# Second-round tiles counted back from the last row, exponentials one beat later, and more identity products in front, in a decoder layer on one Trainium2 core

## The reference

```
x = x + attn(layernorm(x))           # sigmoid q and k, 16 heads of 8, k^T v then q (k^T v); norm, gate, Wo, relu
x = x + xattn(layernorm(x), ctx)     # 16 heads of 64: softmax(q k^T / 8) v, then Wo
x = x + ffn(layernorm(x))            # shared SwiGLU (256 wide) + one of 8 routed SwiGLUs, the one of the largest logit
```

## Time and profile before

| | |
|---|---|
| median of 3 runs | 638.46 us |
| lowest and highest | 635.97 us, 639.41 us |
| the profiled execution | 638.0 us |
| its span, first to last instruction | 636.3 us |
| mean granted TensorE clock | 0.98 |
| PE busy | 584.8 us (92%) |
| ACT busy | 432.4 us (68%) |
| DVE busy | 427.4 us (67%) |
| POOL busy | 311.6 us (49%) |

### The profile page before, as it was taken

How to read it: one execution, slowest core, us unless ns; L and a number is a source line. 1 busy time by engine, 2 the same in 40 slices (tenths; PEclk the granted TensorE clock), 3 DMA queues, 4 the chain that set the end, 5 groups by cost and what they waited for, 6 DMA issues and landing times.

```text
span 636.3 us, 15539 instructions
## 1 busy us (share of the span) xinstructions
PE 584.8 (92%) x5461; PEld 533.8 (84%) x5461; DVE 427.4 (67%) x1183; ACT 432.4 (68%) x1514; POOL 311.6 (49%) x331
## 2 busy tenths in 40 slices
PE   8879999999999999999999999999999997968971
PEld 8767998888889889888988898889899986867971
DVE  4858767776776677676867686768674674865551
ACT  2658778786867686767676877787668766635650
POOL 3544644363446543663366336633752374354543
PEclk9988999999999999999999999999999999999996
DMA  6500000100010001000100000000401112433410
GB/s 156 121 2 13 18 3 1 30 2 2 1 31 18 18 2 31 18 19 1 30 19 18 1 14 18 18 2 1 141 28 38 31 43 68 125 116 105 130 37 8
DMA packets 24956, 23.53 MB, mean 37 GB/s; under 512 B 7007, under 2 KB 22497, under 8 KB 24880
## 3 DMA queue, kind: packets, MB, share of 16 engines
q1 hardware_dynamic: 20368, 14.91, 8.9%
q0 software_dynamic: 2784, 6.32, 2.8%
q10 hardware_dynamic: 1728, 1.32, 0.9%
HBM read 15.03 MB, written 7.95 MB: 36 GB/s over the span
## 4 chain that ended last, share of the span: by engine, by line
PE 59%; ACT 17%; DVE 12%; issue 4%; DMA 2%; POOL 1%; another core or an unknown queue 1%; SPq 1%; ACTq 0%; DVEq 0%; POOLq 0%
PE bank L1314 9%; PE bank L1335 9%; ACT prob L1070 7%; PE bank L1196 7%; PE bank L1324 6%; PE bank L1197 6%; PE bank L1198 6%; PE bank L1346 4%; PE bank L1451 4%; PE bank L1295 2%; PE bank L1203 2%; ACT probT L1076 2%; DVE mneg L842 2%; DMA prob<-in_L_xattn_Wk_dram 2%; ACT L1041 1%
## 5 line engine op out<-in xcount | busy, mean ns | idle before, releaser
L1070 ACT ACTIVATE prob<-bank,mneg 128x128 f32<-128x128 f32 x512 | 182.5, 380 | 92.8 <-DVE mneg L842 92.7
L583 POOL TENSOR_TENSOR prob<-prob,rden 128x512 f32<-128x512 f32 x128 | 130.9, 1043 | 105.9 <-DVE rden L849 105.7
L1070 ACT ACTIVATION_READ_ACCUMULATOR prob<-bank,mneg 128x1 f32 x512 | 111.6, 218 | 0.0
L1076 ACT COPY probT<-bank 128x512 f32<-128x512 f32 x128 | 77.7, 607 | 23.4 <-PE bank L1324 23.0
L842 DVE TENSOR_REDUCE mneg<-bank 128x4 f32<-128x512 f32 x128 | 80.6, 671 | 4.0 <-PE bank L1314 3.1
L1324 PE MATMUL bank<-ident,prob 128*128 128x128 f32 x512 | 79.3, 278 | 3.4 <-POOL prob L583 2.0
L522 POOL TENSOR_TENSOR rstd<-var_eps,neg_half 128x4 f32<-128x4 f32 x24 | 24.7, 1030 | 102.3 <-DVE var_eps L676 102.3
L1324 PEld LDWEIGHTS bank<-ident,prob 128*128 128x128 f32 x512 | 59.7, 143 | 11.4 <-issue 5.5
L1314 PE MATMUL bank<-kT,qT 64*128 64x128 f32 x1024 | 65.8, 278 | 0.3 <-issue 0.3
L859 DVE COPY V<-bank 128x512 f32<-128x512 f32 x62 | 42.7, 689 | 33.2 <-PE bank L1198 31.9
L1314 PEld LDWEIGHTS bank<-kT,qT 64*128 64x128 f32 x1024 | 59.7, 188 | 6.2 <-issue 3.0
(11 more groups left out here) (195 smaller groups left out, 1357.9 us busy)
## 6 DMA issues: line engine op xcount, KB each, us to landing
prob<-routed SPq DMA_DIRECT2D x39, 128.5 KB, 2.1
s_work<-in_x_dram SPq DMA_DIRECT2D x8, 256.0 KB, 3.0
ctx_nat<-in_ctx_dram SPq DMA_DIRECT2D x8, 192.0 KB, 2.5
routed<-blank ACTq DMA_DIRECT2D x8, 128.5 KB
s_work<-in_L_ffn_rt_gate_dram SPq DMA_DIRECT2D x1, 1024.0 KB, 5.5
s_work<-in_L_ffn_rt_up_dram SPq DMA_DIRECT2D x1, 1024.0 KB, 9.5
out_dram<-probT,prob POOLq DMA_INDIRECT x39, 2.6
prob<-in_L_xattn_Wq_dram SPq DMA_DIRECT2D x1, 512.0 KB, 8.4
```

The costliest lines, as they stand in the source:

```text
L583: nc.gpsimd.tensor_tensor(view, view, spread(rden[:, m % 2, c * NC:(c + 1) * NC], 2, S), ALU.mult)\
L1070: last = nc.scalar.activation(prob[:, m % 2, p * S:(p + 1) * S], score_bank[c][:, i * S:(i + 1) * S], ACT.Exp, bias=mneg[:, m % 2, p:p + 1 ...
L1076: nc.scalar.copy(probT[:, m % 2, c * 512:(c + 1) * 512], made(r1, ("T", m, c))[:])\
```

## The change

**Exponentials a beat later.** `exps_of` moves the exponentials of matrix n+1 from beats 0 to 3 of `n` to beats 1 to 3 of `n` and beat 0 of `n+1`; for the last matrix the last two quarters stand in beat 3. ACT's list reads nearly word for word as before, since each beat still has `empty_T` and then four exponentials; what has changed is the quarter that they belong to. DVE takes one quarter's maxima in each beat instead of two in beats 0 and 2, first in beats 1 to 3 and last in beat 0, and its reciprocals go to beat 3 and behind the copies of beat 0. POOL's first two multiplications go from beat 2 to beat 3.

**Second-round tiles.** They are counted back from each region's last row, so that they overlap rows that round 1 has done (written again with equal values) or 128 blank rows in front of the region. The blank rows are written by SP near the front, 9 DMAs where there was 1; the eight of ACT are gone. POOL waits in `write_out(j)` for the write of tile j-4, and at j = 21 for all of round 1.

**ACT in the tiles.** The value that says which expert comes next is read behind the copy, a tile ahead.

**In front**, `stay_awake` gives 9 products instead of 6 in beat 2 of n = -4, and 5 more in beat 3.

```diff
+        def exps_of(n, b):
+            if n + 1 == B - 1 and b == NC - 1:
+                return [(n + 1, NC - 2), (n + 1, NC - 1)]
+            if b > 0:
+                return [(n + 1, b - 1)] * (0 <= n + 1 < B)
+            return [(n, NC - 1)] * (0 <= n < B - 1)
...
# SP
-            sp.dma_start(routed[E * REGION:E * REGION + P, :], blank[:]).then_inc(blank_in, 16)
+            for e in range(E + 1):
+                sp.dma_start(routed[e * REGION:e * REGION + P, :], blank[:]).then_inc(blank_in, 16)
...
             sp.wait_ge(table, TABLE_1)
+            sp.wait_ge(blank_in, 16 * (E + 1))
...
-            sp.wait_ge(blank_in, 16 * (E + 1))
             sp.wait_ge(routed_in[1], 16 * GB * (NG // 2))
...
# POOL
-                    if b == 2 and live(n + 1):
+                    if b == 3 and live(n + 1):
                         norm_probs(n + 1, 0)
                         norm_probs(n + 1, 1)
...
+            def written(j):
+                pool.wait_ge(out_in[j % RING], 16 * (j // RING + 1))
             def write_out(j):
+                if 4 <= j <= ROUND1:
+                    written(j - 4)
+                if j == ROUND1:
+                    for i in range(1, 4):
+                        written(j - 4 + i)
...
# DVE
+                if tiles == ROUND2:
+                    entry(nc.vector.scalar_tensor_tensor(out=first[:, 0:E], in0=ntiles[:], scalar=-float(P),
+                                                         in1=next_row[0:1, :], op0=ALU.mult, op1=ALU.add))
+                    entry(nc.vector.tensor_tensor(stride[:], first[:, 1:], first[:, 0:E], ALU.subtract))
...
-                entry(nc.vector.tensor_tensor(stride[:], first[:, 1:], first[:, 0:E], ALU.subtract))
...
-                    entry(nc.vector.tensor_copy(tail_i[:], next_row[0:1, :]))
...
-                    if b == 0 and live(n):
-                        reciprocal(n, 1)
-                    if (n, b) == (B - 1, 0):
-                        fill_first_table()
-                    if b == 2 and live(n + 1):
+                    if b == 3 and live(n + 1):
                         reciprocal(n + 1, 0)
-                    if b == 2 and live(n + 1):
-                        row_max(n + 1, 2)
-                        row_max(n + 1, 3)
+                    if b > 0 and live(n + 1):
+                        row_max(n + 1, b)
...
+                    if b == 0 and live(n):
+                        reciprocal(n, 1)
+                    if (n, b) == (B - 1, 0):
+                        fill_first_table()
                     if b == 0 and live(n + 1):
                         row_max(n + 1, 0)
-                        row_max(n + 1, 1)
...
# ACT
-            def end_region(e):
-                if e == 0:
-                    act.wait_ge(table, TAILS)
-                tail = act.value_load(tail_i[0:1, e:e + 1], min_val=e * REGION, max_val=e * REGION + TOKENS)
-                act.dma_start(routed[bass.ds(tail, P), :], blank[:]).then_inc(blank_in, 16)
...
-                    if live(n + 1):
-                        exp_chunk(n + 1, b)
+                    for chunk in exps_of(n, b):
+                        exp_chunk(*chunk)
...
+            held = {}
             def copy_weights(j):
                 if j >= 3:
                     act.wait_ge(gu_ready, j - 2)
+                nc.scalar.copy(w4[j % 3], rt_gu[:, bass.ds(held.pop(j) * (2 * I), 2 * I)]).then_inc(w4_in, 1)
+                if j + 1 < TILES:
+                    held[j + 1] = expert_of(j + 1)
...
-                if j in END_STEPS:
-                    end_region(END_STEPS.index(j))
...
# PE
                     if (n, b) == (-4, 2):
-                        stay_awake(6)
+                        stay_awake(9)
+                    if (n, b) == (-4, 3):
+                        stay_awake(5)
```

More of the change, by code:

```diff
@@ L193, in decoder_layer @@
         t_row = sb("t_row", [1, ROUND1])
-        tail_i = sb("tail_i", [1, E], I32)
         row_tab = sb("row_tab", [1, 2, ROUND1], I32)
@@ L353, in decoder_layer @@
         TABLE_STEPS = (7, 8, 10)
-        END_STEPS = range(8, 8 + E)
         S1_BANKS = {"turn x": [(0, "s1_dve")], "project first pair": [(1, "s1_dve"), (2, "s1_dve")],
@@ L428, in decoder_layer @@
         CONSTS = CONSTS_S1 + 14
-        TABLE_1, TAILS, TABLE_2 = 15, 16, 27
+        TABLE_1, TABLE_2 = 14, 27
         gu_bank = score_bank[1:]
@@ L610, in _ @@
             nc.gpsimd.iota(expert_m[:], [[0, GB], [1, E]], base=-E, **ramp).then_inc(consts, 1)
-            nc.gpsimd.iota(next_row[:], [[REGION, E]], base=0, **ramp).then_inc(consts, 1)
+            nc.gpsimd.iota(next_row[:], [[REGION, E]], base=P, **ramp).then_inc(consts, 1)
             nc.gpsimd.memset(blank[:, 0:2 * D], 0.0).then_inc(consts, 1)
@@ L615, in _ @@
             s1(0, "rstd of attention")
-            nc.gpsimd.iota(region[:], [[REGION, E]], base=0, **ramp).then_inc(consts, 1)
+            nc.gpsimd.iota(region[:], [[REGION, E]], base=P, **ramp).then_inc(consts, 1)
             nc.gpsimd.iota(steps[:], [[0, E], [P, TOKENS // P]], base=0, **ramp).then_inc(consts, 1)
@@ L927, in second_table @@
                 if third == 0:
-                    entry(nc.vector.tensor_copy(tail_i[:], next_row[0:1, :]))
-                    assert entries[0] == TAILS
                     entry(nc.vector.tensor_tensor(cnt[:], next_row[0:1, :], first[:, 0:E], ALU.subtract))
@@ L1150, in _, with expert_of @@
                             ffn(g, step)
+            def expert_of(j):
+                if j == ROUND1:
+                    act.wait_ge(table, TABLE_2)
+                half, i = (0, j) if j < ROUND1 else (1, j - ROUND1)
+                return act.value_load(exp_tab[0:1, half, i:i + 1], min_val=0, max_val=E - 1)
+            held = {}
             def copy_weights(j):
@@ L1155, in copy_weights @@
                     act.wait_ge(gu_ready, j - 2)
-                if j == ROUND1:
-                    act.wait_ge(table, TABLE_2)
-                half, i = (0, j) if j < ROUND1 else (1, j - ROUND1)
-                e = act.value_load(exp_tab[0:1, half, i:i + 1], min_val=0, max_val=E - 1)
-                nc.scalar.copy(w4[j % 3], rt_gu[:, bass.ds(e * (2 * I), 2 * I)]).then_inc(w4_in, 1)
+                nc.scalar.copy(w4[j % 3], rt_gu[:, bass.ds(held.pop(j) * (2 * I), 2 * I)]).then_inc(w4_in, 1)
+                if j + 1 < TILES:
+                    held[j + 1] = expert_of(j + 1)
             act.wait_ge(table, TABLE_1)
@@ L1165, in _ @@
             act.wait_ge(wr_in, 16 * 3)
+            held[0] = expert_of(0)
             copy_weights(0)
```

## The result

The changed kernel takes 659.31 us (median; 659.15 to 659.41), the kernel before 638.93 on the same chip (635.97 to 644.00, four runs each). The ratio is 1.032, with an interval of 1.029 to 1.036. The profiled executions have spans of 657.4 and 636.3 us, so 21.1 us are to be found. I look for them with a ruler that costs nothing: the start of T0 (the first turn of a matrix on PE, once in each n), which can be read in both traces, in us.

A forecast was written before the change was run, and what follows sets the result against it. PE was taken to bound the loop, a DMA-ACT-PE chain the tiles, the clock the front. Front -1.4, loop +9.2, tiles -3.6, last steps +0.1 make +4.3 us on 638.0: 642.3, median 642.8; range 631 to 649.

The forecast's parts named there:

- The sign: Whole kernel: the change was forecast to make it slower, by 4.3 us.
- The stall between the halves: Loop, beat 0: PE waits for the fourth quarter's exponentials before the scores' second half; 0.45 to 0.9 us, gross 14.2.
- What vanishes against it: Loop: a later PE finds some present waits over; 5 us taken off, bounds 0 and 9.85.
- rival D: Loop: the copy of V in beat 3 becomes a new wait, some 0.7 us in each of 30 n; 650, chance 0.08.
- The end of the loop: Two quarters of exponentials in beat 3 of n = 30 and the last steps: +0.1 us.
- In front: Ahead of the loop: more identity products raise PE's clock from 0.51 at 34.3 to 37.7 us; -1.4 us, bounds -3 and 0.
- The tiles: Behind the loop: ACT freed of blank DMAs and a table wait; -3.6 us, bounds 0 and -11.
- the first: Tiles: ACT's table wait goes, so PE's step from tile 9 to 10 falls from 3.23 to about 1.5; 1.6 us off.
- the unnamed wait: Tiles: ACT's 4.02 us wait with no releaser named, behind a blank DMA; half of it, 2 us, taken off.
- A: Loop: the stall doesn't bite and the waits vanish; loop -3, the rest -4.9, 630 us, chance 0.14.
- B: Tiles: ACT's unnamed waits, 9.3 us, go with its blank DMAs; tiles -11, 635.4 us, chance 0.12.
- C: Loop nearly neutral: the stall stays but takes up all 9.85 us of idle time; +4, 637.6 us, chance 0.20.

## Why the prediction was right or wrong

The sign was right, the size was not: +4.3 us forecast, about +21 measured, outside the range. Step by step:

**The stall between the halves** was right in place, cause and price. Forecast 0.45, 0 and 0.45 and 0.9 us for the remainders 3, 0, 1 and 2; measured from T0 to T1, +0.53, -0.29, +0.56 and +0.96. The signal that I had guessed at 0.05 us took 0.06. Gross 14.2 us forecast; 16.2 measured, 13.8 from n = 0 to 27 and 2.4 in n = 28 to 30.

**What vanishes against it** was the step that failed. "I take 5" stood for waits that disappear, less nothing for new ones. Measured turn by turn from T0 of n = 0 to T0 of n = 31, 8.5 us vanish and 15.2 us of new waits come, beside the stall: 16.2 + 15.2 - 8.5 is, but for rounding, the 23.0 that the loop lost. (These are sums of the differences between the two kernels over all stretches from one turn to the next: those from T0 to T1 that grew are the stall, the others that grew the new waits.) The step had put 15.2 us at nothing. Where four n lost their 2.28 us, by the starts of the turns:

| stretch | before | after | |
|---|---|---|---|
| T0 to T1, remainders 3, 1, 2 | 18.90 | 20.95 | +2.05, the stall |
| T1 to T2, remainder 2 | 3.28 | 4.31 | +1.03, T2 waits for V |
| T3 to T0, 3 to 0 and 1 to 2 | 6.11 | 6.57 | +0.46, T0 waits for V, for POOL |
| all others | | | -1.26, waits that vanish |

The 8.5 us are more than my 5 and near the upper bound that I had set. Of the 15.2 us, 11.0 lie before n = 28 and 4.2 at the end. I had booked new waits in rival D alone, at 0.08, and there for one copy of V, that of beat 3. The larger wait, at T2, is for the copy of beat 1, where a reduction stands ahead as well, and two blocked instructions of DVE. I had seen that a reciprocal and a reduction stand ahead of V in beat 3, and that POOL's multiplies go a beat later, and costed neither with the slack in hand. That slack could be read for POOL: in remainder 2, before, T0 starts 3.92 us behind POOL's first multiply (325.37 and 329.29). The multiply and the signal need 1.17 of them, which leaves 2.75, and the beat that POOL's multiplies moved by is 3.4 us long there.

**The end of the loop**, from T0 of n = 28 to T0 of n = 31, took 6.6 us. 2.4 of them are the stall, which the 14.2 had in them; the other 4.2, against the +0.1 that I had given, are the waits ahead of the three T0, 3.0 at the last. I had looked at the two quarters in beat 3 and at the scatters' order, not at what stands in POOL's queue ahead of the multiplies when no slack is left: four scatters at 1.27 us each. One edit there gave 2.6 us back, by the profiles.

**In front**: -1.4 forecast. The piece itself gave 1.2, with the clock as foreseen. In the changed kernel it was lost at T0 of n = 0, 0.7 later than before; in the kernel before, by itself, a ratio of 0.998 says that it holds.

**The tiles**: -3.6 forecast, -2.5 on the first chip; on the others, with the old exponentials, the stretch behind T0 of n = 31 went from 92.3 to 91.2 us. Of the two terms, the first was wrong: the step from tile 9 to 10 takes 3.23 us after the change too (579.22 to 582.45), as the product of the shared FFN stands in it (1.95 us, in both kernels). The 2 us for the unnamed wait have no base, since those waits are there without these DMAs on the first chip, and not there with them on another. The real gain was elsewhere, tiles 13 to 18, 9.6 us before and 7.9 with the change, both on chips of the experiments.

**The rivals.** A is refuted: the stall bites, 25 times. B is too. C had the mechanism of the vanishing waits, 8.5 us, and missed the new ones. D had a part of the right cause, too small.

**What stays open**: what the unnamed waits in the tiles of the first chip are; what ACT's delay alone costs with the old order on DVE and POOL; and how much of the wait for V at T2 would stay if only the reduction, or only the blocked instructions, stood ahead of the copy.

## What to carry to other kernels

In a loop that one engine bounds, ask of every moved step not how long others wait for it, but how much slack is left in front of the bounding engine: ACT's 92 us of waiting for maxima went here, and the kernel became 3% slower. When two engines' queues are shifted by a beat, list each chain that ends at the same matmul (here V's bank and exponential, reciprocal, multiply) with its slack before and after, the last pass of the loop by itself. And look at the bounding engine's own small waits first: 0.69 us once in four passes, mended by moving one copy in ACT's list, gave 0.7%, more than the other parts of this change gave together (0.2%).

## What the runs showed that I had not expected

The same program takes 638.9 us on one chip and 620.3 to 621.3 on four others, with T0 of n = 31 within 0.9 us on the two that have a profile of it. The 18 us are all in the tiles, where the first chip's ACT has waits that no semaphore event explains, up to 4.0 us, and where the mean granted clock is 0.91 in the window of the earlier trace rows against 1.00. A DVE instruction on 8 numbers (L939) took 3.05 us beside four multiplies of POOL and ended with them; it took 0.22 in the run with the old exponentials and 0.12 with POOL's last multiplies in beat 2. So it was held while POOL worked; by what was not tried apart.
